# Self-attention in a decoder layer: step pairs added by transfers, a new order and new owners for masks and reciprocals

## What is computed

```python
z = T * sigmoid(x.mean(axis=1) @ span_w + span_b)
scores = einsum('bhtd,bhsd->bhts', q, k) / SCALE
attn = softmax(where(causal, scores, -1e30), axis=-1)
mask = clip((R + z[:, :, None, None] - dist) / R, 0.0, 1.0)
attn = attn * mask
attn = attn / (attn.sum(axis=-1, keepdims=True) + 1e-08)
out = einsum('bhts,bhsd->bhtd', attn, v)
```

## Time and profile before

| | us |
|---|---|
| median of 3 runs (3273.79 to 3278.83) | 3274.09 |
| the profiled execution | 3275.21 |
| its span, first to last instruction | 3272.5 |
| TensorE busy | 2978.1 |
| VectorE busy | 1858.2 |
| ScalarE busy | 1059.7 |
| GpSimd busy | 945.0 |

### The profile page before, as it was taken

How to read it: one execution, slowest core, us unless ns; L and a number is a source line. 1 busy time by engine, 2 the same in 40 slices (tenths; PEclk the granted TensorE clock), 3 DMA queues, 4 the chain that set the end, 5 groups by cost and what they waited for, 6 DMA issues and landing times. The chain is left out here.

```text
span 3272.5 us, 53205 instructions
## 1 busy us (share of the span) xinstructions
PE 2978.1 (91%) x19242; PEld 1667.5 (51%) x19242; DVE 1858.2 (57%) x2220; ACT 1059.7 (32%) x2510; POOL 945.0 (29%) x606
## 2 busy tenths in 40 slices
PE   8999799999999999999999799999999787777878
PEld 6876333333333434333333578888888342332345
DVE  4345878797887878787882345555554510000038
ACT  3222344444444444444444223333333100110123
POOL 0000554445454454444454022222221000000013
PEclk9999799999999999999999799999999898888889
DMA  4553512131312212121200411221221769999954
GB/s 168 180 198 136 130 40 62 53 78 44 71 53 56 69 49 69 46 69 52 62 14 4 158 36 65 67 67 65 69 68 58 256 260 420 420 421 420 421 220 161
DMA packets 181201, 438.25 MB, mean 134 GB/s; under 512 B 17470, under 2 KB 51928, under 8 KB 156457
## 3 DMA queue, kind: packets, MB, share of 16 engines
q1 hardware_dynamic: 174057, 425.19, 37.2%
q10 hardware_dynamic: 6976, 10.75, 0.9%
HBM read 351.74 MB, written 83.89 MB: 133 GB/s over the span
## 5 line engine op out<-in xcount | busy, mean ns | idle before, releaser
L785 ACT ACTIVATE B_e<-B_pS 128x512 f32<-128x512 f32 (+3 forms) x1280 | 617.4, 533 | 826.0 <-PE B_pS L865 425.2
L640 POOL TENSOR_TENSOR B_em<-B_e,B_mask 128x1024 f32<-128x1024 f32 (+1 forms) x320 | 672.2, 2102 | 703.4 <-ACT B_e L785 666.9
L703 DVE TENSOR_REDUCE mx<-B_pM 128x4 f32<-128x2048 f32 (+2 forms) x299 | 588.6, 1968 | 35.1 <-PE B_pM L847 16.7
L865 PE MATMUL B_pS<-B_qs,B_ks 128*128 128x512 f32 (+3 forms) x1280 | 501.3, 445 | 24.0 <-DMA B_qs<-B_mrow 13.9
L696 DVE SCALAR_TENSOR_TENSOR B_em<-B_mask,B_e 128x1024 f32<-128x1024 f32 (+1 forms) x320 | 354.9, 1109 | 237.4 <-PE B_pN L895 235.8
L865 PEld LDWEIGHTS B_pS<-B_qs,B_ks 128*128 128x128 f32 x1280 | 227.0, 191 | 341.8 <-issue 227.0
L883 PE MATMUL B_pD<-B_e,B_tiny 128*32 128x512 f32 (+3 forms) x2560 | 307.0, 552 | 0.0
L889 PE MATMUL B_pD<-B_em,B_ones 128*32 128x512 f32 (+3 forms) x2560 | 297.7, 537 | 0.5 <-DVE B_em L696 0.5
L895 PE MATMUL B_pN<-B_em,B_v 128*32 128x512 f32 (+3 forms) x2560 | 293.9, 531 | 0.0
L2088 PE MATMUL E_pI<-ring,hT 128*32 128x512 f32 x1024 | 184.2, 813 | 100.5 <-DMA ring<-in_L_ffn_e_W_dram 55.7
L2011 DVE TENSOR_TENSOR E_ug<-E_pT,bT 128x32 f32 x32 | 5.7, 192 | 446.3 <-PE E_pT L2098 446.3
(11 more groups left out here) (288 smaller groups left out, 4759.2 us busy)
## 6 DMA issues: line engine op xcount, KB each, us to landing
ring<-in_L_ffn_e_W_dram SPq DMA_DIRECT2D x128, 1024.0 KB, 21.8
ring<-in_L_ffn_e_Wg_dram SPq DMA_DIRECT2D x64, 1024.0 KB, 23.6
B_qs<-q_hi SPq DMA_DIRECT2D x64, 256.0 KB, 4.4
B_ks<-k_hi SPq DMA_DIRECT2D x64, 256.0 KB, 3.9
E_xq<-xT_sc ACTq DMA_DIRECT2D x18, 512.0 KB, 10.2
ring<-x_sc SPq DMA_DIRECT2D x36, 256.0 KB, 2.7
qc<-in_x_dram SPq DMA_DIRECT2D x34, 256.0 KB, 2.7
qc<-a_sc SPq DMA_DIRECT2D x34, 256.0 KB, 3.0
```

The lines of the kernel that those rows point to most:

```text
L640: nc.gpsimd.tensor_tensor(em[:, f % SLOTS_EM, DVE_HEADS:, w0:], e[:, f % SLOTS_E, DVE_HEADS:, w0:], mask[:, DVE_HEADS:, u0:u0 + BLK - w0], ...
L703: nc.vector.tensor_reduce(mx[:, :, qt, c], pM[:, :, 0:w], AX.X, ALU.max).then_inc(max_taken, 1)
L785: nc.scalar.activation(e[:, f % SLOTS_E, h, w0:], pS[:, h % SBANKS, w0:], ACT.Exp, scale=SCALE).then_inc(exp_ready, 1)
L865: last = nc.tensor.matmul(pS[:, h % SBANKS, w0:], ks[:, kb // NT, h, kb % NT * P:(kb % NT + 1) * P], qs[:, qb, h, w0:], start=True, stop=( ...
```

## The change

Everything is in `self_attention`, but for two units of the projection phase.

- **Pairs.** In rows 1 to 3, steps off the diagonal form pairs (a even, a+1): 12 pairs per group. GpSimd issues a transfer with an add, e of a += e of a+1 (`add_pair`, 128 x 8 KB), behind its product of step a+1. It waits for VectorE's and GpSimd's products of step a and the exponentials of a+1. One tiny round, ahead of the ones of step a+2, does for both. e has 5 slots.
- **Order.** VectorE reduces the unit of iteration f before the masked product of step f.
- **Heads.** GpSimd takes heads 0 and 1 and starts when two exponentials are there; VectorE takes heads 2 and 3 and waits for all four. GpSimd caps its own heads' mask once per row (`cap`).
- **Masks.** ScalarE makes the ramps (Relu with the span as bias), 16 per group. Row 0 has a mask tile of its own, mask_row0; a transfer copies it into the first 512 columns of mask (`copy_near`), for which step 5 of the group waits.
- **Reciprocals.** SP packs one row per head of den into 128 x 16, VectorE inverts that, and SP stores it to DRAM and loads it back, spread over 32 partitions per head ("pack" and "spread"). GpSimd's divide comes one step later. The very last row is inverted as before. num has two slots.
- **Smaller.** Scores use rows 0 to 96 of qs and ks, so that only one row of ks is set to one and qs needs no memset. The first loads and constants come in another order. In block 7 of the projections the units stand behind products 1, 3, 4, 6, 7, 9, 10 and 11 in place of 1, 3, 5, 7, 9, 11, 11 and 11. All loops are written out.

The diff, cut:

```diff
-SLOTS_E, SLOTS_EM = 4, 2
+SLOTS_E, SLOTS_EM = 5, 2
+E_KEPT = 3
-DVE_HEADS = 2
+POOL_HEADS = 2
+PAIRS = [f for f, (qb, kb) in enumerate(FLAT) if kb < NT * qb and kb % 2 == 0]
+PAIRED = {f for a in PAIRS for f in (a, a + 1)}
+SUMMED_AFTER = 2
+TINY_AT = {f: [a for a in PAIRS if a + SUMMED_AFTER == f] + [f] * (f not in PAIRED) for f in range(STEPS)}
+RAMP_OWN = {ENDS[c - 1] - NT + h: (c, h) for c in range(2, BPB) for h in range(HPG)}
+RAMP_NEXT = {29 + h: (0, h, 0) for h in range(HPG)}
+RAMP_NEXT.update({38: (1, 0, 0), 39: (1, 1, 0), 0: (1, 2, 2), 1: (1, 3, 2)})
-UNITS_AFTER = {4: [7, 9, 11], 5: [1, 3, 7, 9, 11], 6: [1, 3, 7, 9, 11], 7: [1, 3, 5, 7, 9, 11, 11, 11]}
+UNITS_AFTER = {4: [7, 9, 11], 5: [1, 3, 7, 9, 11], 6: [1, 3, 7, 9, 11], 7: [1, 3, 4, 6, 7, 9, 10, 11]}
...
+                elif kind == "pack":
+                    sp.wait_ge(den_out, row + 1)
+                    at_least(sp, inverse, row)
+                    for h in range(HPG):
+                        sp.dma_start(packed[h * DH:(h + 1) * DH, :], den[h * DH:h * DH + 1, :]).then_inc(den_packed, 16)
+                elif kind == "spread":
+                    sp.wait_ge(inverse, row + 1)
+                    at_least(sp, inv_loaded, 64 * row)
+                    sp.dma_start(inv_sc[row % 2].rearrange("h (j i) -> (h j) i", i=PACK), packed_inv[:, :]).then_inc(inv_stored, 16)
+                    sp.wait_ge(inv_stored, 16 * (row + 1))
+                    at_least(sp, out_ready, row)
+                    for h in range(HPG):
+                        sp.dma_start(inv[h * DH:(h + 1) * DH, :], inv_sc[row % 2, h].partition_broadcast(DH)).then_inc(inv_loaded, 16)
...
-                pool.wait_ge(exp_ready, it * HPG * STEPS + HPG * (f + 1) + SBANKS)
+                pool.wait_ge(exp_ready, HPG * f + POOL_HEADS)
...
+            def add_pair(a):
+                n = PAIRS.index(a % STEPS)
+                pool.wait_ge(masked_dve, a + 1)
+                pool.wait_ge(masked_pool, a + 1)
+                pool.wait_ge(exp_ready, HPG * (a + 2))
+                pool.dma_start(e[:, a % SLOTS_E, :, :], e[:, (a + 1) % SLOTS_E, :, :], accum_op=ALU.add).then_inc(summed[n % 2], 16)
...
-                dve.wait_ge(exp_ready, it * HPG * STEPS + HPG * f + DVE_HEADS + SBANKS)
+                dve.wait_ge(exp_ready, HPG * (f + 1))
...
+                if u < ITS * STEPS:
+                    reduce_unit(u)
+                if f < ITS * STEPS:
+                    weigh(f)
+                if f >= 4 and (f - 4) % STEPS in ENDS:
+                    invert(row_at(f - 4))
```

## The result

| | before | changed |
|---|---|---|
| median, us (6 runs each) | 3276.3 (3273.8 to 3279.2) | 3307.9 (3292.3 to 3316.1) |
| ratio, 95% interval | | 1.0091 (1.0074 to 1.0107) |
| span of the profiled execution | 3272.5 | 3310.9 |
| TensorE busy, whole kernel | 2978.1 | 2950.8 |
| last numerators of self-attention start | 1800.15 | 1833.89 |

The forecast was 3229, faster. The runs of the changed kernel spread over 24 us, those of the one before over 5.

What follows compares the result with a forecast made beforehand. The prediction took TensorE to set the pace. Its terms, 84.5 + 36 + 11 - 18 - 68 = 45.5 us, took the profiled 3275.2 to 3229.7, stated as 3229; the full range was 3143 to 3345, the forecast's own 3190 to 3262.

Steps and rivals of the forecast that it cites:

- What bounds the kernel: Self-attention stage: TensorE sets the pace, busy 174.3 of the 181.55 us of a group of 40 steps.
- Tiny rounds, 84.5 us: TensorE in self-attention: twelve of a group's 40 steps lose a 0.88 us tiny round, saving 84.5 us.
- The group's first stall, 36 us: Where VectorE made the next group's first mask: TensorE's wait and longer products go, 5.2 us seven times, saving 36 us.
- The start, 11 us: Projection stage ends some 5 us earlier, and 6 us kept from four memsets dropped before the first ones: 11 us saved.
- Adding transfers: Paired steps: 7.3 us from issue to landing, three pairs per group late by 1.5 us, costing 18 us in all.
- The two product engines, 68 us: VectorE's and GpSimd's masked products exclude each other after narrow steps and at row entries: 9 us per group, costing 68 us.
- rival C: Slower by the excluded port: GpSimd keeps winning the race in rows 2 and 3, 3282 to 3352 us; chance 0.18.
- The clock: At the group's first stall only: TensorE's first products after the wait run longer, 1.71 us for 0.88.
- D: Slower by late sums: TensorE stands before the tiny round of every second step, 3342 us; chance 0.15.
- the clean 3143: Rival, whole kernel: VectorE's products nearly always first and the sums landed in time, 3143 us; chance 0.26.

Runs made afterwards that it cites:

- b1: The kernel before, with the tiny round of each pair's second step left out and no transfer adding it: 3199.1 us.
- b2: The kernel before, with only block 7's projection units behind products 1, 3, 4, 6, 7, 9, 10 and 11: 3276.2 us, ratio 1.0007.
- a2: The changed kernel without its 96 adding transfers, tiny rounds reading only the first step of each pair: 3240.4 us.
- a6: The changed kernel with GpSimd's division of a finished row, and SP's store with it, two steps later: 3275.8 us.
- a1: The changed kernel with VectorE casting the turned row maxima ahead of the step's masked product, not behind it: 3269.1 us.
- c3: The changed kernel with cast first, division two steps later, GpSimd's cap one step earlier, and next group's key and value loads moved to steps 36 to 44: 3204.1 us.
- c1: The changed kernel with both the cast ahead of the product and GpSimd's division two steps later: 3230.1 us, 0.988 of before.
- g1: c3 with GpSimd's product of step 13 held until VectorE's product of step 12 is done: 3213.6 us.
- g2: g1 with TensorE's transposition of the row maxima behind the second pair of scores instead of ahead of it: 3221.8 us.
- f1: The changed kernel with adding transfers of half the size (128 x 4 KB, heads 0 and 1 only): 3237.3 us.
- a3: The changed kernel without pairs: a tiny round in every step and no adding transfer: 3290.6 us.

## Why the prediction was wrong

By its own steps:

- **What bounds the kernel**: right. TensorE sets the pace, and every loss showed as one of its waits or as its clock.
- **Tiny rounds, 84.5 us**: right in the count, and 75 us when done alone (b1).
- **The group's first stall, 36 us**: it is gone (VectorE's reduces are in no list of TensorE's waits). I took the gain for free. But its place was taken at once by two waits of 2.2 to 2.5 us per group for the cast.
- **The start, 11 us**: 3. The first ones start at 350.22, 353.37 before; the projection part gave nothing (b2). The rest of the 7 us from the memsets went into the wait for the first loads of q, 10.3 us.
- **Adding transfers**: the landing time was nearly right, 7.7 us for 7.3 (GpSimd's issue, 0.5 of the sum, takes 0.9). By the Trainium skill, *DMA: Bandwidth & Descriptors*, "Anatomy of one DMA — SWDGE (gpsimd) path", and *Collectives: The Full Stack*, "Stop ④", the estimate was 6.8; the measurement is above both. Their price of 18 us was wrong: 68 (a2). The step that failed looked only at TensorE's wait for the sum, and gave the reciprocals' hops "two steps each", some 6 us for the last two, at no cost. It left out that the hops share the DMA engines with the adding transfers. A 1 MB transfer in front makes the 8 KB store 5.8 us instead of 1.4, and where one is issued right ahead of the loads, a load takes up to 8.1 us for 2.0; GpSimd waits in its queue. "If late, it holds GpSimd's product" was said and priced at 1 to 2 us; it cost 32 us (a6).
- **The two product engines, 68 us**: the mechanism and its places (just after narrow steps, at the entries of rows 1 to 3) were right, and "VectorE's product also delays the cast of the maxima behind it" was even said, at 3 us for each of two entries per group. The size was wrong. At these two entries the wait for the cast is 2.2 to 2.5 us and the clock falls behind it for 3.4 or 6.8 us, a further 1.7 to 3.4. TensorE's waits for the cast and for either engine's product are 76 us in all, with 150 us at the lower clock behind them: some 140 us for my 68 (half of what TensorE works at the lower clock is counted), a part of it the late reciprocals' doing. a1, which moves only the cast, gives 39 us back. The long run of collisions of rival C, on the other hand, isn't what cost: c3 has as many and is 104 us faster.
- **The clock**: the term that was missing. The forecast had it in one place, where it goes. I should have asked of each new wait what the clock does behind it: 167 us at the lower level instead of 37 cost 58 us, two thirds of what the tiny rounds save.

The forecast's 3229 is what c1 gives (3230), with two faults mended that it priced too low. The agreement is of totals and not of terms: c1 waits 31.2 us for sums, where the forecast had 18 for them with all that follows. The range of 3143 to 3345 holds the measured 3308 only because rivals of both signs were in it. Two slips in its arithmetic change nothing: 96 x 2.1 is 202 and not 199, and C's worst case of 3352 lies outside the range. Of the rivals, C (slower by the excluded port) had the sign but the wrong place, and D (late sums) named the part that cost 68 us, at 199; they were given 0.33 together. I held them apart, though late reciprocals, which the transfers cause, also make GpSimd run two products beside VectorE's (the rows at 1051.33). Why is c3 61 us above the clean 3143? Its waits for VectorE's products and for the sums (27.0 + 9.7), the start (8) and the end of the phase (3) make 48 of it, and the 21 us that TensorE works at the lower clock another 10. That is a sum of rows and not a test; g1 and g2 show that single waits don't come off it.

## What to carry to other kernels

Before moving work on an engine, list what is queued behind it and who needs that soonest: a 0.3 us cast behind a 1.2 us product cost 39 us (a1), while in c3 all collisions of that product leave TensorE 27 us of waits for it. Price a wait of the bounding engine with what its clock does afterwards, not at its own length. A transfer that is in time for its own consumer can still be late for others': look at every small transfer that is issued next to it, and at the queue of the engine that waits for that one. And look for the second fault before judging the first mend: the cast, with some 90 us at stake, gave 39 alone and 46 on top of the later division (3275.8 to 3230.1), and other waits grew in its place.

## What the runs showed of the hardware

- **The clock falls at short waits.** The last wait of TensorE before one fall was of 1.58 us (a row of TensorE, and a window of 4 us whose clock is 0.58):

```profile
960.94 1.93 PE L931 MATMUL B_pD<-B_em,B_ones 128*32 128x512 f32 x8 [1.58 <-DVE B_em L743]
```

```profile
960.00:964.00 4.00, 3.06 (x16) 0.67 (x16) 4.00 (x3) 0.28 (x1) 0.90 (x1) 0.58 0.50 99
```

  The stretches at 1.2 GHz were 3.4, 6.8 or 10.2 us. A wait of the same length that ended at 778.47 was followed by none, so the length of the last wait alone doesn't tell.
- **Small transfers land behind a big one.** The 8 KB store of the reciprocals took 5.8 us in the median with adding transfers of 1 MB, 2.8 with 512 KB (f1) and 1.4 without (a2).
- **A transfer with an add inside SBUF**, 128 x 8 KB: 7.7 us in the median, 0.9 us of GpSimd to issue it; 4.6 us for 128 x 4 KB.
- **Who starts first doesn't always win.** In a1 VectorE's product began 0.45 us ahead of GpSimd's division, and still took 5.40 us, until the division and the product behind it were done. Why is open; it began during GpSimd's issue of a transfer, which alone stretches nothing (1.21 us at 1059.43 in c3, beside an issue from 1059.21).

```profile
553.60 0.90 POOL L702 DMA_DIRECT2D B_e<-B_e  x1 [1.38 <-ACT B_e L804]
553.83 5.40 DVE L743 SCALAR_TENSOR_TENSOR B_em<-B_mask,B_e 128x1024 f32<-128x1024 f32 x1
554.28 1.55 POOL L711 TENSOR_TENSOR B_ao<-B_num,B_inv 128x512 f32<-128x512 f32 x1
...
555.54 2.60 POOL L694 TENSOR_TENSOR B_em<-B_e,B_mask 128x1024 f32<-128x1024 f32 x1
```

- **The end of a phase costs more when GpSimd has issued transfers in it.** GpSimd's first work of the next phase waited 6.51 us for the barrier; in f1, with half the bytes, 6.51 too; in the kernel before and in a2, a3 and b1, all without adding transfers, 3.2 or 3.3:

```profile
1846.20 0.21 POOL L47 MEMSET W_ident<- 128x128 f32 x1 [6.51 <-POOLq L2414]
```
